# Turning the leftover pairs of an interaction buffer: four whole-array transposes in place of half-array ones

## The reference, cut to what matters

```
e = stack([tbl_f[ids[:, f]] for f in range(26)], axis=1)
combined = concatenate([e, dense[:, None, :]], axis=1)        # 2048 x 27 x 128
interact = einsum('bfd,bgd->bfg', combined, combined)
z = interact[:, triu_i, triu_j]                               # 351 pairs
h = concatenate([z, dense], axis=1)                           # 479 columns
h = maximum(h @ W_top1 + b_top1, 0)                           # 512
h = maximum(h @ W_top2 + b_top2, 0)                           # 256
y = h @ W_top3
```

## Time and profile before

| | |
|---|---|
| three runs | 380.94, 385.37, 389.42 us, median 385.37 |
| the profiled execution | 381.75 us, of which the span is 380.0 |
| PE busy | 355.5 us (94%), mean granted clock 0.996 |
| POOL busy | 262.5 us (69%) |
| DVE busy, ACT busy | 221.2 us (58%), 172.1 us (45%) |

### The profile page before, as it was taken

The page is one execution under the profiler, slowest core; times in us unless marked ns, Lnnn a source line. Parts: engine busy times, 40 slices in busy tenths (PEclk is TensorE's granted clock), DMA queues, the critical chain, the costliest instruction groups (busy, mean ns, idle before and its releaser), DMA issues.

```text
span 380.0 us, 14533 instructions
## 1 busy us (share of the span) xinstructions
PE 355.5 (94%) x6528; PEld 326.6 (86%) x6528; DVE 221.2 (58%) x246; ACT 172.1 (45%) x445; POOL 262.5 (69%) x280
## 2 busy tenths in 40 slices
PE   2987979999999999999999999999999999999987
PEld 2776978989989898999989899998999899988876
DVE  5695898954569534774367626674367636632122
ACT  2437335364635353463535454463535444354522
POOL 6676787777777777777677777767777777777100
PEclk9998999999999999999999999999999999999999
DMA  6877414333222323223232323222223232222000
GB/s 179 237 205 227 130 47 138 80 85 79 71 80 57 82 67 73 66 59 78 60 84 58 80 57 91 59 72 85 72 58 78 51 85 64 59 57 54 24 2 2
DMA packets 17615, 31.26 MB, mean 82 GB/s; under 512 B 5776, under 2 KB 8720, under 8 KB 17552
## 3 DMA queue, kind: packets, MB, share of 16 engines
q0 software_dynamic: 8704, 17.84, 18.4%
q1 hardware_dynamic: 7920, 11.68, 10.5%
q10 hardware_dynamic: 928, 0.80, 0.7%
HBM read 30.29 MB, written 0.01 MB: 80 GB/s over the span
## 4 chain that ended last, share of the span: by engine, by line
PE 84%; DMA 7%; DVE 3%; ACT 3%; issue 2%; SPq 0%; DVEq 0%; ACTq 0%
PE x_ps L635 37%; PE tail_ps L717 16%; PE gram_ps L654 13%; PE x_ps L616 8%; DMA hot_in<-in_tbl 7%; PE tail_ps L684 3%; PE tail_ps L694 2%; DVE onehot L900 2%; PE tail_ps L693 1%; PE tail_ps L690 1%; DVE hot_lo L886 1%; ACT xt L394 1%; ACT xt L849 1%; PE x_ps L758 1%; PE tail_ps L666 1%
## 5 line engine op out<-in xcount | busy, mean ns | idle before, releaser
L599 POOL DMA_INDIRECT raw<-in_tbl,ids_sb x272 | 261.6, 962 | 90.3 <-issue 80.7
L900 DVE TENSOR_TENSOR onehot<-ids_wide,row_ps 128x1024 fp32r<-128x1024 int16 (+1 forms) x160 | 179.6, 1164 | 59.4 <-PE x_ps L635 56.2
L635 PE MATMUL x_ps<-onehot,hot_hi 128*128 128x256 f32 x566 | 144.6, 291 | 4.4 <-DVE onehot L900 1.5
L635 PE MATMUL x_ps<-onehot,hot_lo 128*128 128x256 f32 x566 | 139.0, 282 | 0.3 <-issue 0.3
L635 PEld LDWEIGHTS x_ps<-onehot,hot_hi 128*128 128x128 f32 x566 | 106.6, 188 | 6.9 <-ACT xt L394 3.5
L635 PEld LDWEIGHTS x_ps<-onehot,hot_lo 128*128 128x128 f32 x566 | 106.7, 189 | 0.7 <-issue 0.6
L394 ACT COPY xt<-x_ps 128x256 f32<-128x256 f32 x72 | 49.0, 680 | 79.0 <-PE x_ps L635 78.9
L654 PE MATMUL gram_ps<-xt 128*27 128x26 f32 x4096 | 56.0, 192 | 5.6 <-ACT xt L849 1.2
L654 PEld LDWEIGHTS gram_ps<-xt 128*27 128x27 f32 x4096 | 46.0, 104 | 15.7 <-issue 8.2
L849 ACT COPY xt<-x_ps 128x384 f32<-128x384 f32 (+1 forms) x80 | 44.4, 629 | 0.8 <-PE x_ps L616 0.8
L416 ACT COPY gram<-gram_ps 128x416 f32<-128x416 f32 (+1 forms) x32 | 16.2, 506 | 57.2 <-PE gram_ps L654 57.2
(11 more groups left out here) (95 smaller groups left out, 347.8 us busy)
## 6 DMA issues: line engine op xcount, KB each, us to landing
raw<-in_tbl,ids_sb POOLq DMA_INDIRECT x272, 2.6
ids_wide<-in_hot_ids SPq DMA_DIRECT2D x17, 256.0 KB
hot_in<-in_tbl SPq DMA_DIRECT2D x14, 256.0 KB, 3.5
weights_in_place<-in_w SPq DMA_DIRECT2D x12, 128.0 KB, 2.5
hot_in<-in_tbl SPq DMA_DIRECT2D x4, 320.0 KB, 3.8
dense_sb<-in_dense_t ACTq DMA_DIRECT2D x6, 128.0 KB, 2.4
dense_sb<-in_dense_t SPq DMA_DIRECT2D x2, 128.0 KB, 3.3
ids_wide<-in_hot_ids SPq DMA_DIRECT2D x1, 192.0 KB
```

What stands on the lines that cost most here:

```text
L599: nc.gpsimd.indirect_dma_start(out=raw[k][:, f, :], out_offset=None, in_=sources[f], in_offset=bass.IndirectOffsetOnAxis(ap=ids_sb[:, t, f ...
L635: last = nc.tensor.matmul(ps, table[:, chunk_at[j] + c, :], moving[:, c - a, :], start=(c == 0 and table is tables_of[0]), stop=(c == chun ...
L900: nc.vector.tensor_tensor(columns(p), ids_wide[:, it // IDS % IDS_RING, it % IDS, 0:width].unsqueeze(1).to_broadcast([P, n, width]), row_n ...
```

## The change

The 13 even features are divided: ten lead features (`lead_of`) with exactly 128 pairs in each half, and three others (`REST`, numbers 0, 5 and 12, with 25, 15 and 1 pairs). The lead pairs fill columns 0 to 127 of `z` for both halves. The other pairs of the two halves go side by side: those of the upper half from column 128, those of the lower half from column 182, and the pairs of a feature with its own neighbour stand at 169 to 181 of the upper half. Step ("zt", 1) then turns columns 118 to 222 by four transposes with all 128 rows, 105 columns wide; its output has 512 columns, of which each half's own 256 are read. `pairs_copy` needs two copies in place of one for each of the three features, and `zt_parts` gives two parts in place of one for step ("zt", 1), so L461 and L493 become two instructions each there. `z` grows from 192 to 223 columns for each sample, DVE clears all of it at the start, and PE's wait for the clearing goes. The rows of `W_top1` are put in the new order on the host.

```diff
+REST = (0, 5, 12)
...
-    pair_start = [sum(shared_len[:i]) for i in range(len(shared_len) + 1)]
-    half_pairs = [pair_start[-1] + len(shared_len), pair_start[-1]]
+    n_shared = sum(shared_len)
+    rest_of = REST
+    lead_of = [c for c in range(len(shared_len)) if c not in rest_of]
+    pair_start = {c: sum(shared_len[i] for i in lead_of if i < c) for c in lead_of}
+    rest_start = {c: P + sum(shared_len[i] for i in rest_of if i < c) for c in rest_of}
+    alone_start = n_shared
+    half_pairs = [n_shared + len(shared_len), n_shared]
+    z_rest = [half_pairs[0] - P // 2, half_pairs[0]]
+    z_wide = half_pairs[0] + n_shared - P
...
-    z_wide = P + P // 2
...
             for c, q in enumerate(of):
                 src = ps[:, c * P:(c + 1) * P].rearrange("g (s p) -> g s p", s=QUAD)[:, :, q + 2:feats]
-                copy(z[:, :, pair_start[q // 2]:pair_start[q // 2 + 1]], src)
+                n = shared_len[q // 2]
+                if q // 2 in lead_of:
+                    copy(z[:, :, pair_start[q // 2]:pair_start[q // 2] + n], src)
+                else:
+                    for odd, shift in enumerate((0, z_rest[1] - P)):
+                        rows = slice(odd * groups_block, (odd + 1) * groups_block)
+                        at = rest_start[q // 2] + shift
+                        copy(z[rows, :, at:at + n], src[rows])
...
         def zt_parts(j, ps, of):
...
+            turned_z = ps.rearrange("p (s o g) -> p o g s", s=QUAD, o=2)
             if j == 0:
-                return (ps.rearrange("p (s o g) -> p o g s", s=QUAD, o=2),
-                        of[:, 0:2, :].rearrange("p o (g s) -> p o g s", s=QUAD))
-            return (ps[0:kz[2], 0:BLOCK].rearrange("p (s g) -> p g s", s=QUAD),
-                    of[0:kz[2], 2, :].rearrange("p (g s) -> p g s", s=QUAD))
+                return [(turned_z, of[:, 0:2, :].rearrange("p o (g s) -> p o g s", s=QUAD))]
+            rest = of[:, 2, :].rearrange("p (g s) -> p g s", s=QUAD)
+            return [(turned_z[a:b, odd], rest[a:b]) for odd, (a, b) in enumerate(((0, P // 2), (P // 2, kz[2])))]
...
-                src, hi = zt_parts(j, ps, zt_hi)
-                copy(hi, src).then_inc(zt_rounded, 1)
+                for src, hi in zt_parts(j, ps, zt_hi):
+                    last = copy(hi, src)
+                last.then_inc(zt_rounded, 1)
...
-                (src, hi), (_, lo) = (zt_parts(j, tail_ps[bank], of) for of in (zt_hi, zt_lo))
-                nc.vector.tensor_tensor(lo, src, hi.bitcast(F32), ALU.subtract).then_inc(zt_split, 1)
+                for (src, hi), (_, lo) in zip(*(zt_parts(j, tail_ps[bank], of) for of in (zt_hi, zt_lo))):
+                    last = nc.vector.tensor_tensor(lo, src, hi.bitcast(F32), ALU.subtract)
+                last.then_inc(zt_split, 1)
...
-                            pe.wait_ge(z_padded, 1)
...
-                    upper, lower = slice(0, groups_block), slice(groups_block, P)
+                    cols = slice(0, P) if j == 0 else slice(z_rest[0], z_wide)
                     for s in range(QUAD):
-                        if j == 0:
-                            last = nc.tensor.transpose(ps[:, s * P:(s + 1) * P], z[:, s, 0:P], ident[:, :])
-                        else:
-                            of_s = slice(s * groups_block, (s + 1) * groups_block)
-                            nc.tensor.transpose(ps[0:P // 2, of_s], z[upper, s, P:z_wide], ident[upper, upper])
-                            last = nc.tensor.matmul(ps[P // 2:kz[2], of_s], z[lower, s, P:half_pairs[1]],
-                                                    ident[lower, lower], start=True, stop=True)
+                        last = nc.tensor.transpose(ps[0:kz[2 * j], s * P:(s + 1) * P], z[:, s, cols], ident[:, :])
...
-            nc.vector.memset(z[0:groups_block, :, half_pairs[0]:z_wide], 0.0).then_inc(z_padded, 1)
+            nc.vector.memset(z[:, :, :], 0.0)
```

More of the change, by code:

```diff
@@ L94, in build @@
     shared_len = [feats - 2 - q for q in range(0, feats - 1, 2)]
-    pair_start = [sum(shared_len[:i]) for i in range(len(shared_len) + 1)]
-    half_pairs = [pair_start[-1] + len(shared_len), pair_start[-1]]
+    n_shared = sum(shared_len)
[7 more added lines that the diff above has]
+    z_wide = half_pairs[0] + n_shared - P
+    assert sum(shared_len[c] for c in lead_of) == P and z_rest[0] <= P
     col_groups = [list(range(q, min(q + 8, feats - 1), 2)) for q in range(0, feats - 1, 8)]
     assert (feats - 1) % 2 == 0
-    z_wide = P + P // 2
-    assert sum(half_pairs) == pairs and P < half_pairs[1] <= half_pairs[0] <= z_wide
+    assert sum(half_pairs) == pairs
     n_zt = 2
@@ L344, in build @@
         weights_split = sem("weights_split")
-        z_padded = sem("z_padded")
         zt_rounded = sem("zt_rounded")
@@ L427, in pairs_copy @@
                 src = ps[:, c * P:(c + 1) * P].rearrange("g (s p) -> g s p", s=QUAD)[:, :, q + 2:feats]
-                copy(z[:, :, pair_start[q // 2]:pair_start[q // 2 + 1]], src)
+                n = shared_len[q // 2]
[6 more added lines that the diff above has]
+                        copy(z[rows, :, at:at + n], src[rows])
             at = ps[0:groups_block, of[0] + 1:of[0] + 2]
             src = bass.AP(at.tensor, at.offset, [at.ap[0], (SLOTS, QUAD), (P + 2, len(of))])
-            place = pair_start[-1] + of[0] // 2
+            place = alone_start + of[0] // 2
             return copy(z[0:groups_block, :, place:place + len(of)], src)
         def zt_parts(j, ps, of):
+            turned_z = ps.rearrange("p (s o g) -> p o g s", s=QUAD, o=2)
             if j == 0:
-                return (ps.rearrange("p (s o g) -> p o g s", s=QUAD, o=2),
-                        of[:, 0:2, :].rearrange("p o (g s) -> p o g s", s=QUAD))
-            return (ps[0:kz[2], 0:BLOCK].rearrange("p (s g) -> p g s", s=QUAD),
-                    of[0:kz[2], 2, :].rearrange("p (g s) -> p g s", s=QUAD))
+                return [(turned_z, of[:, 0:2, :].rearrange("p o (g s) -> p o g s", s=QUAD))]
+            rest = of[:, 2, :].rearrange("p (g s) -> p g s", s=QUAD)
+            return [(turned_z[a:b, odd], rest[a:b]) for odd, (a, b) in enumerate(((0, P // 2), (P // 2, kz[2])))]
         def y_copy(act, h, ps):
@@ L958 @@
     start = [i * (n_tables + 1) - i * (i + 1) // 2 for i in range(n_tables + 1)]
+    lead = [n for n in range(0, n_tables, 2) if n // 2 not in REST]
+    rest = [n for n in range(0, n_tables, 2) if n // 2 in REST]
     def row_of(a, b):
         return start[min(a, b)] + abs(a - b) - 1
-    halves = [[row_of(order[n + h], b) for n in range(0, n_tables, 2) for b in order[n + 2:]] for h in range(2)]
-    halves[0] += [row_of(order[n], order[n + 1]) for n in range(0, n_tables, 2)]
-    pair_rows = [halves[0][:P], halves[1][:P], halves[0][P:], halves[1][P:]]
+    lead_rows, rest_rows = ([[row_of(order[n + h], b) for n in of for b in order[n + 2:]] for h in range(2)]
+                            for of in (lead, rest))
+    rest_rows[0] += [row_of(order[n], order[n + 1]) for n in range(0, n_tables, 2)]
+    pad = [P // 2 - len(rest_rows[0]), P // 2 - len(rest_rows[1])]
     w1 = np.asarray(inputs["W_top1"])
@@ L975 @@
         "hot_ids": np.ascontiguousarray(rows_of_ids).view(np.int16)[:, ::2],
-        "w1": np.concatenate([np.pad(w1[rows_of], ((0, -len(rows_of) % (P // 2)), (0, 0))) for rows_of in pair_rows]
-                             + [w1[sum(map(len, pair_rows)):]]),
+        "w1": np.concatenate([w1[lead_rows[0]], w1[lead_rows[1]], np.pad(w1[rest_rows[0]], ((pad[0], 0), (0, 0))),
+                              np.pad(w1[rest_rows[1]], ((0, pad[1]), (0, 0))), w1[start[-1]:]]),
         "b1": np.asarray(inputs["b_top1"]).reshape(-1, P).T,
```

## The result

The changed kernel takes 380.12 us (median of 20 runs, 376.79 to 382.64), the kernel before 382.88 (20 runs, 380.94 to 389.42). The ratio is 0.9928, 95% interval 0.9899 to 0.9957: 2.8 us faster, 1.6 to 3.9. The execution that was profiled is the slowest of the 20, 382.64 us with a span of 380.8, so its span isn't to be set against that of before; its inner lengths are.

A forecast was written before the change was run, and what follows sets the result against it. PE and POOL's gathers were taken to bound the kernel together, PE one microsecond behind. -1.1 - 1.19 + 0.16 + 0.86 = -1.27 from 381.75 gives 380.5; allowing for the runs' median, 382.3, range 376.5 to 387.0.

The forecast's parts named there:

- Two bounds, PE one microsecond behind: At the last turn (tile 15) PE and POOL's gathers end together, with PE having 1.1 us to spare.
- Where the waits fall: Late tiles: PE begins to wait for gathers at tile 11, 1.2 us at tile 13, 3.1 at tile 15.
- a sign of being wrong: POOL's last gather, expected near 352.6: starting several us earlier or later would make the prediction wrong.
- The step, 1.63 to 0.44, saving 1.19: Step ("zt", 1) in each of eight blocks: four transposes replace twelve half-array instructions, saving 1.19 us (1.1 to 1.3).
- -1.1 at the last turn: Before the last turn: of 8.3 us saved in seven blocks only 1.1 us comes out, between 0 and 1.3.
- -1.03 in the last tail: Last tail of block 7: the eighth step's saving of 1.19 us, less 0.16 for a copy of ACT.
- the extra copy of ACT: Last tail, between the first and third cols steps: feature 0's second copy costs 0.16 us, up to 0.27.
- The clock, +0.86: Behind the last turn: the new wait of some 3 us lowers PE's clock, costing 0.86 us, between 0 and 1.72.
- The median: Runs' median 385.37: 384.1 if POOL's gathers were later, 380.5 if PE was later; the middle, 382.3, taken.
- The block 6 wait: Block 6, where h1 follows zt at once: PE's wait there comes off the wait at tile 15.
- The layout's copies: Between blocks ACT's three more copies, 0.5 us a block, cost nothing because PE's surplus takes them in.
- the rival of a step that gets no cheaper: Zt's second step: pieces overlap or whole transposes cost as much; only copies and clock remain, 381.9 us; chance 0.04.

The follow-up runs named there:

- fewer gathers: One of 17 tables gathered for tiles 0 and 1 only (14 of 272 gathers left out): kernel before 380.01 us, changed kernel 373.46 us.
- PE made dearer: Kernel before with zt's half-array step done twice: 397.0 us; changed kernel with zt's four new transposes done three times: 382.26 us.
- an earlier wait of POOL: POOL waits before each sixth gather for the one five before, not each eighth for three before: kernel before 382.06 us, changed kernel 375.88 us.
- POOL held up: Four small clearings of a spare tile on POOL ahead of each tile's gathers: kernel before 401.92 us, changed kernel 402.01 us.
- the layout alone: New columns and double copies, but the twelve half-array instructions and one rounding, 14 gathers left out: 381.50 us, 0.9993 of the kernel before.

## Why the prediction was right

The main step was right: the gathers cap the gain. Forecast 382.3 (376.5 to 387.0), measured 380.12; forecast within 2%, measured 0.7% faster. Point by point:

- *Two bounds, PE one microsecond behind.* Shown four ways: fewer gathers take 2.6 us off the kernel before and 6.7 off the changed one (373.46 against 380.12); PE made dearer is paid in full before and a third after; an earlier wait of POOL gives about 1 us before (0.28%, and the interval takes in no gain) and 4.2 after; and POOL held up moves both by 20.
- *Where the waits fall.* The prediction let PE's savings pile up against 3.0 us to spare and put the first wait at tile 11, 1.2 us at tile 13 and 3.1 at tile 15. In the trace PE waits from tile 3 on, 1.2 to 1.6 us each time, because the gathers of that execution were 2.9 us later there: before the change PE had 3.3 us to spare at tile 3 (the eighth of the eleven transposes from 98.46 starts at 99.38, the gather lands at 96.13), and the later gathers and one saving used that up. From there to tile 9 each block's saving became a wait, which is the mechanism that was forecast. But the last gather started 3.1 us later than in the trace before, and a start several us later is what the prediction had put down as a sign of being wrong. POOL's own waits, which it took as given, differ from trace to trace (6.2 to 13.7 us with the wait before each eighth gather).
- *The step, 1.63 to 0.44, saving 1.19.* In block 4 1.19 (2.16 to 0.97), in the last tail 1.14 (2.07 to 0.93), 0.7 to 1.1 a block in the middle. That the half-array pieces of this kernel run one after the other is borne out: had they overlapped, as the prediction reads the rule on independent tiles in the Trainium skill (TensorEngine Tiling (Array Packing), Tiling Modes, Key Properties), nothing could have come out with fewer gathers. Both pieces of a pair write the same PSUM bank here; no run has them in two, so whether that is why they don't overlap stays open.
- *-1.1 at the last turn and -1.03 in the last tail.* The whole from the last gather's start to the end fell by 2.34 in the profiled executions, against 2.13 without the clock: 1.10 ahead of gram, as forecast, and 1.24 behind it. Inside the second the extra copy of ACT was undersized: the first cols steps lie 1.76 apart (365.47 to 367.23) in place of 1.41 (363.59 to 365.00 in the trace before), 0.35 against the 0.16 given. Smaller steps that were not forecast made up for it (from gram to the first cols step 0.16 less, behind zt 0.28 less).
- *The clock, +0.86.* This term was mis-sized. Behind the last wait of 1.22 us the windows of the changed kernel's trace stand at 1.00 to the end; 0 was the end of the range that held there. The sum without it, -2.1, is nearer to the -2.8 measured. The wait was sized at 3.1 us and came to 1.22, since PE had lost time elsewhere (last section). With the waits of over 4 us, in the kernels held up, the clock falls, and the ends are longer by more than the 0.86. The windows around the wait:

```profile
356.00:360.00 4.00, 2.37 (x63) 1.80 (x63) 0.00 (x0) 1.72 (x5) 0.72 (x1) 1.00 0.13 33
360.00:364.00 4.00, 3.71 (x194) 3.22 (x182) 1.02 (x2) 0.50 (x1) 0.00 (x0) 1.00 0.02 4
```

- *The median.* The forecast went out from 385.37 and took the middle between two readings of the runs' spread. Over 20 runs the median of before is 382.88, 2.5 lower; the middle comes down by half of that, to 381.0, and without the clock's 0.86 to 380.2. That this meets the 380.12 so closely is luck in part: the two readings lie 1.1 us apart, and the runs of one kernel up to 8.5. The longest runs of before, up to 389.42, have no match after the change (at most 382.64), which fits time lost on PE's side that its new room takes in; no trace of such a run was taken, so that stays argued.
- *The block 6 wait.* The prediction said that what PE waits there comes off the wait for the gathers. So it does in the changed kernel; with the gathers out of the way it costs 1.0 us. Mending it in the version with POOL's earlier wait would by itself bring little, since PE comes to the last gather there just as it lands; the gathers would have to come earlier as well.
- *The layout's copies.* Nothing between the blocks: shown by the trace with the layout alone. Their price in all stays open: 0.35 in the last tail by the trace, 1.5 to 2.6 by the times.
- *A slip in the sums.* The price of the rival of a step that gets no cheaper, 381.9, has the copy in it and not the clock, which its sentence names; with both it would be 382.8. Nothing else hangs on it.

## What to carry to other kernels

Before costing an edit on the busiest engine, look for a second engine whose idle time is all issue: it runs at a pace of its own, and its busy share (69% here) hides that. Set the arrival of its last transfer beside its use, here 1.1 us apart; that slack, and what stands behind that point, is all that a saving can bring. To get the rest, move the other engine's own waits: here 1.8% came from both together, where the two alone gave 0.7% and 0.3% (the latter not clear of none).

## What the runs showed of the hardware that was not expected

**A wait without a releaser.** In the changed kernel's trace PE stops once for 1.89 us in the middle of a piece of one-hot products whose operands were all there, and the trace names only issue. The row, with the granted clock of the two windows around it:

```profile
238.85 0.37 PE L651 MATMUL x_ps<-onehot,hot_hi 128*128 128x256 f32 x1 [1.89 <-issue]
```

```profile
236.00:240.00 4.00, 2.01 (x23) 1.79 (x14) 0.00 (x0) 0.51 (x1) 3.09 (x4) 0.79 0.28 73
240.00:244.00 4.00, 3.91 (x119) 3.67 (x119) 3.17 (x3) 1.42 (x3) 3.08 (x4) 0.78 0.20 53
```

The clock fell there, in the middle of the kernel, and PE lost over 3 us in that block (46.4 us between two zt steps where its neighbours take 43). It cost nothing in the end: PE still had to wait 1.22 us for the last gather.

The stop is not alone, and the DMA packets say what goes with it. Among them are some fifty transfers of 16 KB on a queue that the page calls instruction; one of them runs from 236.38 to 237.40, into the stop, and PE goes on 1.4 us after its end. DMA queues in the window 236.3 to 237.5:

```profile
q8 instruction: 1, 0.02, 5.3%
```

Over the eleven traces, from 35 us on, PE stops 19 times for 0.5 us or more with only issue as the releaser and no wait for a gather or for `z` behind it, among them the 1.65 us of the kernel with the transposes done three times. In all 19 it goes on 1.2 to 1.6 us after the end of such a transfer. So it seems to have run out of instructions; no run changes when they are fetched, so this is not shown.

**Twelve small instructions against four large ones.** A transpose of 64 rows and an identity matmul of 64 rows in two instructions take 0.41 us as a pair, as long as almost four whole transposes of 0.11.
